# One product per group statistic, an early SiLU table, a second bank for small products, one spreading pass and a new order in a fused convolution, attention and expert kernel

## The chip, the cores and the metric

The kernel runs on one core of one Trainium2 chip. The metric is the device time of one execution in microseconds (us). The kernel before takes 160.03 us, the median of 3 runs (159.5 to 160.67).

## The reference, cut to what matters

The input x is (16, 64, 16, 16) in float32. Two layers follow each other, each added to its input:

```python
# layer 0: split-attention convolution
x = silu(conv1x1(group_norm(hidden, 32)));  x = silu(conv3x3_grouped(group_norm(x, 16)))
x = group_norm(x, 2)
a = silu(conv(max_over_radix(mean_over_8x8_windows(x)))); a = conv(group_norm(a, 8))
out = hidden + group_norm(einsum(x * softmax_over_radix(a), weight), 32)
# layer 1, attention: causal online-softmax average over the 16 images, scores from tanh(fc(LN(h)))
# layer 1, experts: per token 8 experts of three 64 x 64 layers (batch norm folded, relu),
#   summed with softmax(mean(x) @ Wr) as weights, plus the weighted output biases bo
```

## The kernel before, in words

The 16 images are 8 pairs (2 images x 64 channels fill the 128 partitions), worked in two halves k = 0 and 1 of 4 pairs. Every engine runs its own instruction stream. All five streams are written by one list, `ORDER` (L67): each name in it is a stage, and each engine issues its own part of a stage when it comes to that name, so that one entry sets the place of a step on PE, DVE, ACT and POOL at once. Nothing else orders the work; semaphores make each instruction wait for its inputs.

The stages that the text speaks of:

- `warm` and `heat` (L807 to L817): two PE products each on a block of zeros, whose result nobody reads. 16 and 12 of them.
- `gn1`, `gn2`, `gn4`: statistics over channel pairs. `channel_stats` (L494) takes BN_STATS of 4 images on DVE and squares the means; `moments_product` (L785) sums over partitions on PE in four products (L793, L796) into the bank SMALL; `group_finish` (`gn1f`, ...; L473) copies the result on DVE and makes the variance; POOL raises it to the power -0.5 (L312); `group_shift` (L483) makes the offset.
- `gn3`, `gna`, `w2`, `w3`: small products of the window branch, also into SMALL. Each waits until the reader of the one before in `ORDER` has freed the bank (`small`, L774).
- `xnorm`: DVE normalises x (L516), PE makes the 1x1 convolution (L823). `silu0` (L340) is its activation. `norm0`: DVE writes the padded image (L528).
- `conv.0` to `conv.17`: nine taps for each half on PE (L862); `silu.0` to `silu.7` the activations on ACT (L348), `ws` the window sums on DVE (L570) and the sums of squares on ACT (L356).
- `ynorm.0` to `ynorm.3` (L370): ACT normalises four images of y each. `gate` (L618, L623): DVE multiplies by the window weights. `outp` (L874): the output product on PE. `x1` (L377, L633): the residual on ACT and DVE. `tok` (L879): to tokens, centred.
- `ln1`, `hn`, `hch` (L898), `fc` (L904), `score` (L912), `coef`, `att`, `scan`, `cen`, `ln2`, `xt`: attention. `t2`: the context turned back, in the bank TURN (7).
- `l1` (L992), `l2` (L1005), `d1`: the expert layers, 16 duos of experts, their relus on ACT (L428, L436) and for ten halves on DVE (L710).
- `logits`, `wt`, `wb` (L965): routing weights, their transpose on PE, and their spreading to partitions in four products for each pixel half q (L967), copied by ACT (L445). `mix` (L741 on DVE, L1022 on PE): the weighted third layer; before the first `mix` of each q, two products add the biases (L1021). `finish` (L749): the last addition, then the store.

Of the kernel before, what the change touches and what calls it, by code (L numbers as in the profile page):

```python
# [22 lines left out]
ALU = mybir.AluOpType  # L23
# [5 lines left out]
P = 128  # L29
B, C, S = 16, 64, 16  # L30
# [13 lines left out]
STRIP = 32  # L44
EPS = 1e-5
# [13 lines left out]
def columns(cols=COLS):  # L59
# [12 lines left out]
    heat.0 heat.1 w3.0 ws.7 heat.2 heat.3 outp.0 wan.0 gate.0 gate.1 gn4.0 gn4f.0 gn3.1 gn3f.1 x1.0 heat.4 heat.5 win.1 heat.6 tok.0 ln1.0
    heat.7 ln1.1 ynorm.2 w2.1 heat.8 heat.9 heat.10 hn.0 hch.0 hch.1 fc.0 fc.1 hn.1 score.0 gna.1 coef.0 cen.0 att.0 gnaf.1 scan.0 wan.1
    cen.1 ynorm.3 ln2.0 gate.2 w3.1 gate.3 ln2.1 outp.1 xn2.0 xt.0 heat.11 gn4.1 xn2.1 gn4f.1 d1.0 l1.0 xt.1 x1.1 t2.0 l1.1 d1.1 l2.0
    ln1.2 d1.2 ln1.3 tok.1 l1.2 l2.1 t2.1 hn.2 l1.3 l2.2 d1.3 hch.2 xr.0 l1.4 hn.3 hch.3 fc.2 fc.3 xr.1 d1.4 coef.1 att.1 score.1 scan.1
# [7 lines left out]
def conv_attention_experts(nc: bass.Bass, x: bass.AP, params: bass.AP, row_params: bass.AP, conv1_w: bass.AP, out: bass.AP):  # L83
# [6 lines left out]
    with ExitStack() as ctx:  # L90
# [118 lines left out]
        logits_ready, wexp_ready, wt_ready = sem_list("logits_ready", "wexp_ready", "wt_ready")  # L209
        z1_done, h1_ready, h1_by_dve, z2_done = sem_list("z1_done", "h1_ready", "h1_by_dve", "z2_done")  # L210
# [78 lines left out]
        def _(sp):  # L289
# [41 lines left out]
        def _(act):  # L331
# [111 lines left out]
            def weights_copy(q):  # L443
                act.wait_ge(small_ready, SMALL_AT["wb", q])
                A.activation(wb[:, q], bank[SMALL][:].rearrange("p (e n) -> p e n", e=EP), ACT.Copy).then_inc(small_free, 1)  # L445
# [3 lines left out]
                      "xt": x_copies, "spr": lambda k: spread_first_scales(), "l1": relu1, "l2": relu2, "wb": weights_copy}  # L449
            act.wait_ge(early_params_loaded, 16)  # L450
# [7 lines left out]
        def _(dve):  # L458
# [14 lines left out]
            def group_finish(name, n, rows=P, unit=1.0):  # L473
# [678 lines left out]
```

## Time and profile before

| what | us |
|---|---|
| median of 3 runs | 160.03 |
| the profiled execution's own time | 161.2 |
| its span | 159.4 |
| around the span | 1.8 |
| first product of `conv.0` | 20.19 |
| last `conv` done, `silu.4` starts | 40.97 |
| `outp.0` starts | 51.63 |
| `tok.0` starts | 59.65 |
| `outp.1` starts | 83.06 |
| `l1.0` starts | 89.24 |
| last addition (`finish.3`) starts | 156.13 |

The rows give engine times in one profiled execution. An engine's "busy" is the time in which it has an instruction at work, and the chain of waits is the run of work, followed back from the last instruction, that nothing else could have shortened.

### The profile page before, as it was taken

The page shows a single profiled execution, that of the slowest core. Times are in us where ns is not written, and L with a number is a line of the kernel's source. Part 1 is how long each engine was busy: PE and PEld are TensorE (multiplying, and loading weights), DVE is VectorE, ACT ScalarE, POOL GpSimd, SP SyncE. Part 2 cuts the span into 40 slices and gives each one's busy share as a digit, 9 for nine tenths or more (in the row PEclk, how much of TensorE's full clock was granted, in tenths as well). Part 3 has the DMA queues.
Part 4 walks back from the last instruction along what each step waited for, and adds up shares of the span by engine and source line. Part 5 has one row for each costly group of instructions (what it writes and reads, how often), then busy time and mean ns, then how long its engine had stood idle before and what let it go on. Part 6 is the DMA issues. An engine that isn't in the chain of part 4 may idle for free.

```text
span 159.4 us, 2638 instructions
## 1 busy us (share of the span) xinstructions
PE 136.9 (86%) x981; PEld 65.4 (41%) x985; DVE 101.5 (64%) x297; ACT 77.3 (48%) x161; POOL 31.0 (19%) x28
## 2 busy tenths in 40 slices
PE   6997699999318759778869999999999999999991
PEld 2552344344114228348543652466525252222230
DVE  0766574763545663525988479739886449999531
ACT  0009041670797041668030498844588899661400
POOL 7050612004040060700444206100350000000000
PEclk9999999999956975998775999999999999999999
DMA  4980000000000000000000000000000000002222
GB/s 122 405 329 3 0 4 2 4 0 4 2 0 0 0 0 0 0 0 4 0 2 0 0 0 4 0 0 0 0 4 0 0 4 2 0 0 66 70 66 66
DMA packets 3740, 4.63 MB, mean 29 GB/s; under 512 B 208, under 2 KB 3408, under 8 KB 3600
## 3 DMA queue, kind: packets, MB, share of 16 engines
q1 hardware_dynamic: 3584, 4.27, 7.6%
q10 hardware_dynamic: 144, 0.20, 0.6%
q8 instruction: 8, 0.13, 0.4%
q14 instruction: 4, 0.03, 0.1%
HBM read 3.42 MB, written 1.05 MB: 28 GB/s over the span
## 4 chain that ended last, share of the span: by engine, by line
PE 67%; DVE 15%; ACT 11%; POOL 3%; issue 3%; ACTq 0%; POOLq 0%
PE bank L862 11%; PE bank L1022 9%; PE bank L992 8%; PE bank L1005 8%; PE bank L810 4%; PE bank L874 4%; DVE ctxs L685 4%; PE bank L879 3%; ACT y L370 2%; PE bank L912 2%; PE bank L904 2%; ACT x L377 2%; PE bank L793 2%; PE bank L796 2%; DVE y L623 2%
## 5 line engine op out<-in xcount | busy, mean ns | idle before, releaser
L862 PE MATMUL bank<-pad,w 32*64 32x512 f32 x288 | 17.7, 595 | 1.7 <-DVE pad L528 1.7
L1005 PE MATMUL bank<-h,f2s 64*64 64x512 f32 x128 | 17.2, 609 | 0.0
L992 PE MATMUL bank<-xs,f1s 64*64 64x512 f32 x128 | 17.0, 602 | 0.1
L428 ACT ACTIVATE h<-bank,s_bnb 128x512 f32<-128x512 f32 x22 | 14.5, 693 | 3.4 <-PE bank L992 3.4
L810 PE MATMUL bank<-warm 128*128 128x512 bf16 x31 | 9.8, 474 | 1.4 <-POOL warm L314 1.3
L862 PEld LDWEIGHTS bank<-pad,w 32*64 32x64 f32 x288 | 6.8, 130 | 9.8 <-issue 8.9
L348 ACT ACTIVATE y<-bank,par 128x512 f32<-128x512 f32 x8 | 4.9, 686 | 10.9 <-PE bank L862 10.9
L817 PE MATMUL bank<-warm 128*128 128x512 bf16 x21 | 7.7, 497 | 2.8 <-ACT y L348 2.4
L710 DVE TENSOR_SCALAR h<-bank,s_bnb 128x512 f32<-128x512 f32 x10 | 7.5, 747 | 1.1 <-PE bank L992 1.1
L570 DVE TENSOR_REDUCE s_wst<-y 128x8 f32<-128x512 f32 x8 | 5.5, 684 | 4.1 <-ACT y L348 4.0
L934 PE MATMUL bank<-ctxs,par 128*128 128x128 f32 x32 | 6.3, 323 | 1.2 <-DVE ctxs L685 1.2
L340 ACT ACT_TABLE_LOAD x1 | 1.3, 1283 | 12.2 <-PE bank L823 12.2
L992 PEld LDWEIGHTS bank<-xs,f1s 64*64 64x64 f32 x128 | 4.1, 131 | 7.1 <-ACT h L428 4.3
L874 PE MATMUL bank<-y,par 128*64 128x512 f32 x16 | 5.8, 844 | 1.4 <-DVE y L623 1.4
L741 DVE TENSOR_TENSOR y<-y,wb 128x512 f32<-128x512 f32 x8 | 4.9, 683 | 3.3 <-ACT wb L445 3.3
L879 PE MATMUL bank<-par,x 128*128 128x128 f32 x32 | 5.8, 356 | 1.1 <-DVE x L633 0.9
L879 PEld LDWEIGHTS bank<-par,x 128*128 128x128 f32 x32 | 5.3, 261 | 2.9 <-ACT x L377 2.9
L356 ACT ACTIVATE more<-y 128x256 f32<-128x256 f32 x16 | 6.5, 417 | 0.0
L1005 PEld LDWEIGHTS bank<-h,f2s 64*64 64x64 f32 x128 | 3.6, 131 | 6.5 <-issue 3.2
L810 PEld LDWEIGHTS bank<-warm 128*128 128x128 bf16 x32 | 3.7, 124 | 6.0 <-issue 3.3
L685 DVE SCALAR_TENSOR_TENSOR ctxs<-ctxs,s_coefa 128x64 f32<-128x64 f32 x30 | 6.0, 275 | 0.0
L934 PEld LDWEIGHTS bank<-ctxs,par 128*128 128x128 f32 x32 | 4.6, 206 | 3.4 <-DVE ctxs L685 3.4
(251 smaller groups left out, 268.7 us busy)
## 6 DMA issues: line engine op xcount, KB each, us to landing
par<-params SPq DMA_DIRECT2D x1, 1516.0 KB, 8.8
xin<-x SPq DMA_DIRECT2D x4, 256.0 KB, 4.2
out<-act SPq DMA_DIRECT2D x4, 256.0 KB, 2.2
row_par<-row_params SPq DMA_DIRECT2D x2, 160.0 KB, 8.5
w<-conv_w SPq DMA_DIRECT2D x1, 288.0 KB, 5.0
par<-params ACTq DMA_DIRECT2D x1, 193.5 KB, 3.8
```

Source lines behind the costliest of these rows:

```text
L428: A.activation(h1[(2 * m + h) % 4][:], bank[Z1[h]][:], ACT.Relu, bias=tile("bnb", P, 3 * EP)[:, col:col + 1]).then_inc(h1_ready, 1)
L685: V.scalar_tensor_tensor(ctxs[:, k, q, t], before, a_[:, q, t:t + 1], ctxs[:, k, q, t], ALU.mult, ALU.add).then_inc(ctx_ready, 1)
L710: V.tensor_scalar(h1[(2 * m + 1) % 4][:], bank[Z1[1]][:], tile("bnb", P, 3 * EP)[:, col:col + 1], 0.0, ALU.add, ALU.max).then_inc(h1_by_dv ...
L810: T.matmul(bank[TURN][:], warm[:, 0:P], warm[:], start=True, stop=True)
L817: T.matmul(bank[Z1[0]][:], warm[:, 0:P], warm[:], start=True, stop=True)
L862: ins = T.matmul(bank[CONV1[k][2 * j + h]][at:at + C, :], w1[rows, tap, :], pad[rows, b:b + 2, dy:dy + S, dx:dx + S], start=(tap == 0), st ...
L874: ins = T.matmul(bank[CHAIN[k][j]][h * C:(h + 1) * C, :], w("weight")[:, j * C:(j + 1) * C], y[:, b + 2 * h:b + 2 * h + 2, :], start=True, ...
L879: return T.matmul(bank[CHAIN[k][q]][:, i * P:(i + 1) * P], x1[:, k * PK + i, q * P:(q + 1) * P], w("centre"), start=True, stop=True)
L934: ins = T.matmul(bank[CHAIN[k][q]][:, i * P:(i + 1) * P], w("ident"), pair_of(ctxs, k, q, i), start=False, stop=(i == PK - 1))
L992: ins = T.matmul(bank[Z1[h]][to, :], f1s[own, e, to], xs[own, k, q], start=True, stop=True)
L1005: ins = T.matmul(bank[Z2[h]][at:at + C, :], f2s[rows, h, e, :], h1[(2 * m + h) % 4][rows, :], start=True, stop=True)
L1022: T.matmul(bank[OUT[k][q]][h * C:(h + 1) * C, :], wo[:, e, :], held[mixes[m]], start=False, stop=(e == EP - 1)).then_inc(mlp_done, 1)
```

## The change: what it does

Seven edits.

1. `moments_product`: one product of 24 columns (L814 in the changed kernel) in place of four. DVE writes the squared means over the counts of BN_STATS, and `moments_finish` makes the sums with two TENSOR_REDUCE from the bank in place of one copy.
2. ACT runs a SiLU of one column on a constant before it waits for anything of the parameters, so that the table load stands at the start of its stream.
3. `gn3.1`, `w2.1`, `gna.1` and `w3.1` go to the bank TURN with semaphores of their own.
4. `wb`: one pass of eight products, which alternate between q = 0 (partitions 0 to 31, bank SMALL) and q = 1 (partitions 32 to 63, bank TURN). The rows of parameters lie in four strips of 32 partitions in place of two: two more DMAs, and the transposed weights are 128 wide.
5. The biases of both q are added ahead of the first `mix`, four products from four strips into four banks. The first `mix` waits for both spread weights.
6. `ORDER` is new.
7. `STATS_AT` counts by `win` and `wan`, which follow from 6.

```diff
-    warm.0 warm.1 silu0.0 silu0.1 warm.2 spr.0 warm.3 warm.4 warm.5 warm.6 gn1.0 warm.7 warm.8 gn1.1 warm.9 gn1f.0 warm.10 gn1f.1 warm.11
+    silu0.0 warm.0 warm.1 warm.2 warm.3 silu0.1 warm.4 spr.0 warm.5 gn1.0 warm.6 warm.7 warm.8 warm.9 gn1f.0 gn1.1 xnorm.0 warm.10 warm.11
...
-                ins.then_inc(moments_ready, 1)
-                dve.wait_ge(moments_ready, MOMENTS_AT[name])
-                means = raw.rearrange("p n (a t) -> p n a t", a=2)[:, :, :, 1]
-                V.scalar_tensor_tensor(sq, means, float(HALF_PIX), means, ALU.mult, ALU.mult).then_inc(stats_ready, 1)
+                step(ins)
+                parts = raw.rearrange("p n (a t) -> p n a t", a=2)
+                V.scalar_tensor_tensor(parts[:, :, :, 0], parts[:, :, :, 1], float(HALF_PIX), parts[:, :, :, 1],
+                                       ALU.mult, ALU.mult).then_inc(stats_ready, 1)
...
+                V.tensor_reduce(ms[:, 0, :], sums[:, :, :, 1], AX_X, ALU.add)
+                V.tensor_reduce(ms[:, 1, :], sums[:, :, :, 0:3:2], AX_XY, ALU.add).then_inc(small_free, 1)
...
+            act.wait_ge(consts_ready, 1)
+            A.activation(tile("unused", P, 1), minus_half[:, 0:1], ACT.Silu)
             act.wait_ge(early_params_loaded, 16)
...
-            def weights_spread(q):
-                small(("wb", q))
-                pe.wait_ge(rows_loaded, 32)
+            def weights_spread():
+                small(("wb", 0))
+                pe.wait_ge(ctx_added, Q * NK)
+                pe.wait_ge(rows_loaded, 16 * STRIPS)
                 for e in range(EP):
-                    at = (q * EP + e) * P
-                    ins = T.matmul(bank[SMALL][:, e * P:(e + 1) * P], r_("sel")[:, at:at + P], tile("wT", NK * STRIP, P)[0:STRIP], start=True, stop=True)
-                ins.then_inc(small_ready, 1)
+                    for q in range(Q):
+                        at = (q * EP + e) * P
+                        turned = tile("wT", P, P)[q * STRIP:(q + 1) * STRIP]
+                        ins = T.matmul(bank[(SMALL, TURN)[q]][:, e * P:(e + 1) * P], r_("sel", q)[:, at:at + P], turned, start=True, stop=True)
+                ins.then_inc(spread_done, 1)
...
-                if m % (NK * PER_OUT) == 0:
+                if m == 0:
...
+                    pe.wait_ge(wb_ready, Q)
```

What the new order does to ACT between the activations of half 0 and `outp.0`. Before (`y<-bank` is `silu`, `more,s_wsum` the squares, `y<-y` is `ynorm`, `s_wt` the tanh of `w3.0`):

```order
L348 ACTIVATE y<-bank,par 128x512 x4
L356 ACTIVATE more,s_wsum<-y 128x256 x8
L348 ACTIVATE y<-bank,par 128x512 x3
L356 ACTIVATE more,s_wsum<-y 128x256 x2
L362 ACTIVATE s_wth<-s_wh 64x32
L356 ACTIVATE more,s_wsum<-y 128x256 x2
L370 ACTIVATE y<-y,s_gn3v0nb,s_gn3v0r 128x256 x4
L348 ACTIVATE y<-bank,par 128x512
L356 ACTIVATE more,s_wsum<-y 128x256 x2
L370 ACTIVATE y<-y,s_gn3v0nb,s_gn3v0r 128x256 x4
L383 ACTIVATE s_wt<-bank 128x32
```

and now:

```order
L357 ACTIVATE y<-bank,par 128x512 x4
L365 ACTIVATE more,s_wsum<-y 128x256 x8
L380 ACTIVATE y<-y,s_gn3v0nb,s_gn3v0r 128x256 x4
L357 ACTIVATE y<-bank,par 128x512 x3
L365 ACTIVATE more,s_wsum<-y 128x256 x2
L372 ACTIVATE s_wth<-s_wh 64x32
L365 ACTIVATE more,s_wsum<-y 128x256 x2
L357 ACTIVATE y<-bank,par 128x512
L365 ACTIVATE more,s_wsum<-y 128x256 x4
L380 ACTIVATE y<-y,s_gn3v0nb,s_gn3v0r 128x256 x4
L394 ACTIVATE s_wt<-bank 128x32
```

The first `ynorm` has moved ahead of `silu.4`, and the squares of `silu.7` ahead of the tanh.

PE from the end of `conv` to `tok.0`. Before:

```order
L804 MATMUL bank<-s_wmax,par 64x16 x2
L782 MATMUL bank<-s_wr,par 64x16
L817 MATMUL bank<-warm 128x512 x4
L804 MATMUL bank<-s_wan,w3d 128x16 x2
L817 MATMUL bank<-warm 128x512 x4
L874 MATMUL bank<-y,par 64x512 x4
L793 MATMUL bank<-s_gn4v0raw,par 128x8 x2
L796 MATMUL bank<-s_gn4v0rsq,par 128x4 x2
L782 MATMUL bank<-s_wsum,par 128x16
L817 MATMUL bank<-warm 128x512 x6
L879 MATMUL bank<-par,x 128x128 x8
```

and now:

```order
L825 MATMUL bank<-s_wmax,par 64x16 x2
L814 MATMUL bank<-s_wr,par 64x16
L814 MATMUL bank<-s_wsum,par 128x16
L825 MATMUL bank<-s_wan,w3d 128x16 x2
L895 MATMUL bank<-y,par 64x512 x4
L814 MATMUL bank<-s_gn4v0raw,par 128x24
L838 MATMUL bank<-warm 128x512 x6
L825 MATMUL bank<-s_wmax,par 64x16 x2
L838 MATMUL bank<-warm 128x512 x4
L900 MATMUL bank<-par,x 128x128 x8
```

The eight `heat` products ahead of `outp.0` (L874, now L895) are gone, and ten stand between it and `tok.0` (L879, now L900), where six stood.

PE from the transpose of the routing weights on. Before (`s_wsoft` the transpose, `s_wT` with 128x128 the spreading, with 128x512 the biases):

```order
L960 MATMUL bank<-par,s_wsoft 64x128
L945 MATMUL bank<-par,ctxs 128x128 x4
L1005 MATMUL bank<-h_2,f2s 64x512 x2
L1005 MATMUL bank<-h_3,f2s 64x512 x2
L992 MATMUL bank<-xs,f1s 64x512 x4
L967 MATMUL bank<-s_wT,row_par 128x128 x4
L1005 MATMUL bank<-h_0,f2s 64x512 x2
L1005 MATMUL bank<-h_1,f2s 64x512 x2
L992 MATMUL bank<-xs,f1s 64x512 x4
L967 MATMUL bank<-s_wT,row_par 128x128 x4
```

and now:

```order
L981 MATMUL bank<-par,s_wsoft 128x128
L1029 MATMUL bank<-h_0,f2s 64x512 x2
L1029 MATMUL bank<-h_1,f2s 64x512 x2
L991 MATMUL bank<-s_wT,row_par 128x128 x8
L1016 MATMUL bank<-xs,f1s 64x512 x4
L1029 MATMUL bank<-h_2,f2s 64x512 x2
L1029 MATMUL bank<-h_3,f2s 64x512 x2
L1042 MATMUL bank<-s_wT,row_par 128x512 x4
L1043 MATMUL bank<-y,par 64x512 x4
```

The two spreadings stand as one block, and one `l1` and one `l2` stand between it and the biases.

## Rows read from the trace of the kernel before

**Rows 1.** The page, part 1: busy time of each engine, share of the span, instructions.

```profile
PE 136.9 (86%) x981; PEld 65.4 (41%) x985; DVE 101.5 (64%) x297; ACT 77.3 (48%) x161; POOL 31.0 (19%) x28
```

**Rows 2.** Windows: from:to, length, busy us of each engine, granted clock, DMA, GB/s.

```profile
41.00:51.63 10.63, 4.27 (x17) 2.35 (x19) 6.14 (x17) 9.69 (x30) 1.63 (x1) 0.68 0.00 1
...
89.24:156.13 66.89, 66.03 (x458) 27.40 (x457) 48.89 (x113) 42.68 (x73) 7.48 (x5) 1.00 0.04 13
```

**Rows 3.** The chain of waits up to `conv.0`: start us, us, engine, what, line.

```profile
1.32 5.67 PE bank L810 x14
...
10.94 1.14 PE bank L823 x2
...
12.15 1.28 ACT L340
...
15.72 0.58 PE bank L793 x4
16.30 0.46 PE bank L796 x4
...
17.43 1.00 POOL s_gn2v0r L312
...
20.19 4.56 PE bank L862 x80
```

**Rows 4.** Timeline up to 14 us: start, us, engine, line, operation, out<-in, releaser.

```profile
3.25 0.52 SPq L294 DMA_DIRECT2D par<-params  x1
...
4.73 1.41 DVE L501 BATCH_NORM_STATS2 s_gn1v0raw<-xin 128x6 f32<-128x256 f32 x4 [4.73 <-DMA xin<-x]
...
11.64 1.38 DVE L516 TENSOR_SCALAR xnorm<-xin,s_gn1v1r,s_gn1v1nb 128x256 f32<-128x256 f32 x4
```

**Rows 5.** The page, part 6: DMA issues, KB each, us from issue to landing.

```profile
par<-params SPq DMA_DIRECT2D x1, 1516.0 KB, 8.8
```

**Rows 6.** The chain of waits from the last `conv` to `x1.0`.

```profile
40.97 1.84 ACT y L348 x3
...
44.52 1.96 ACT y L370 x4
...
47.05 0.80 ACT more L356 x4
...
51.63 2.15 PE bank L874 x8
...
57.66 1.49 ACT x L377 x3
```

**Rows 7.** Windows of PE alone: busy (instructions), granted clock, DMA.

```profile
44.00:50.50 6.50, 3.35 (x12) 0.50 0.00 0
...
81.50:88.00 6.50, 5.39 (x16) 0.50 0.00 1
```

**Rows 8.** Timeline: offsets of `gn3.0` and `gn3.1`, `tok.0`, `fc`, `outp.1`, `tok.1`.

```profile
38.84 0.17 DVE L486 SCALAR_TENSOR_TENSOR s_gn3v0nb<-s_gn3v0ms,s_gn3v0r 128x8 f32<-128x8 f32 x1 [1.75 <-POOL s_gn3v0r L312]
...
59.65 3.78 PE L879 MATMUL bank<-par,x 128*128 128x128 f32 x16 [0.85 <-DVE x L633]
59.97 0.16 DVE L486 SCALAR_TENSOR_TENSOR s_gn3v1nb<-s_gn3v1ms,s_gn3v1r 128x8 f32<-128x8 f32 x1
...
69.15 1.97 PE L904 MATMUL bank<-xnorm,par 128*128 128x512 f32 x4
...
83.06 3.68 PE L874 MATMUL bank<-y,par 128*64 128x512 f32 x8 [0.90 <-DVE y L623]
...
93.45 2.05 PE L879 MATMUL bank<-par,x 128*128 128x128 f32 x16 [0.21 <-ACT x L377]
```

**Rows 9.** The chain of waits ahead of `l1.0`, and after 127 us (spreading, biases).

```profile
88.00 0.52 PE bank L817
...
127.74 1.08 PE bank L967 x8
...
133.66 1.06 PE bank L1021 x4
```

More of the change, by code:

```diff
@@ L72 @@
[L72 to L75, printed above, removed]
@@ new lines @@
+    gn1f.1 gn2.0 warm.12 warm.13 gn2f.0 silu.0 bn.0 warm.14 warm.15 xnorm.1 silu.1 norm0.0 silu.2 conv.0 conv.1 conv.2 bnf.0 conv.3 conv.4
+    silu.3 gn2.1 conv.5 conv.6 gn2f.1 conv.7 norm0.1 ws.0 ws.1 ws.2 ws.3 conv.8 ynorm.0 s1row.0 conv.9 silu.4 silu.5 conv.10 conv.11
+    s2row.0 conv.12 gn3.0 conv.13 conv.14 gn3f.0 silu.6 win.0 conv.15 conv.16 conv.17 ws.4 w2.0 ws.5 silu.7 ws.6 gna.0 gnaf.0 ws.7 gn3.1
+    wan.0 gn3f.1 gate.0 ynorm.1 gate.1 w3.0 win.1 outp.0 gn4.0 gn4f.0 heat.0 heat.1 ynorm.2 x1.0 heat.2 w2.1 heat.3 ln1.0 heat.4 tok.0
@@ new lines @@
+    heat.5 heat.6 gna.1 heat.7 heat.8 ln1.1 ynorm.3 hn.0 heat.9 hn.1 hch.0 hch.1 fc.0 fc.1 coef.0 score.0 att.0 cen.0 heat.10 heat.11
+    heat.12 gnaf.1 scan.0 wan.1 cen.1 ln2.0 w3.1 heat.13 gate.2 gate.3 ln2.1 outp.1 xn2.0 xt.0 gn4.1 xn2.1 l1.0 gn4f.1 d1.0 xt.1 x1.1 t2.0
+    l1.1 l2.0 tok.1 d1.1 xr.0 ln1.2 d1.2 ln1.3 l1.2 l2.1 l1.3 d1.3 xr.1 hn.2 hn.3 d1.4 l2.2 l1.4 hch.2 hch.3 t2.1 fc.2 fc.3 score.1 coef.1
+    l2.3 cen.2 cen.3 att.1 scan.1 d1.5 l2.4 l1.5 ln2.2 t2.2 d1.6 xn2.2 ln2.3 d1.7 xr.2 d1.8 l1.6 xn2.3 l2.5 l1.7 d1.9 xt.2 l2.6 l1.8 t2.3
@@ L213, in conv_attention_experts, with positions, small_of @@
         mlp_done, res_ready = sem_list("mlp_done", "res_ready")
-        def positions(names):
-            found = [s for s in ORDER if s[0] in names]
+        def positions(names, without=()):
+            found = [s for s in ORDER if s[0] in names and s not in without]
             return {s: i + 1 for i, s in enumerate(found)}
-        SMALL_AT = positions({"gn1", "gn2", "s1row", "s2row", "gn3", "w2", "gna", "w3", "gn4", "score", "logits", "wt", "wb"})
-        MOMENTS_AT = positions({"gn1", "gn2", "gn4"})
-        STATS_AT = positions({"gn1", "gn2", "gn3", "w2", "gna", "w3", "gn4"})
+        second = [s for s in ORDER if s[1] == 1 and s[0] in ("gn3", "w2", "gna", "w3")]
+        SMALL2_AT = {s: i + 1 for i, s in enumerate(second)}
+        SMALL_AT = positions({"gn1", "gn2", "s1row", "s2row", "gn3", "w2", "gna", "w3", "gn4", "score", "logits", "wt", "wb"}, set(second) | {("wb", 1)})
+        def small_of(name):
+            if name in SMALL2_AT:
+                return bank[TURN], small2_ready, small2_free, SMALL2_AT[name]
+            return bank[SMALL], small_ready, small_free, SMALL_AT[name]
+        given = positions({"gn1", "gn2", "gn3", "win", "gna", "wan", "gn4"})
+        STATS_AT = {({"win": "w2", "wan": "w3"}.get(name, name), k): n for (name, k), n in given.items()}
         var_tiles, VAR_AT, at = {}, {}, 0
@@ L380, in radix_tanh @@
             def radix_tanh(k):
-                act.wait_ge(small_ready, SMALL_AT["w3", k])
-                A.activation(tile(f"wt{k}", P, BK * WIN), bank[SMALL][:, 0:BK * WIN], ACT.Tanh, scale=0.5).then_inc(small_free, 1)
+                area, ready, free, at = small_of(("w3", k))
+                act.wait_ge(ready, at)
+                A.activation(tile(f"wt{k}", P, BK * WIN), area[:, 0:BK * WIN], ACT.Tanh, scale=0.5).then_inc(free, 1)
             def squares(n):
@@ L752, in _ @@
             stages = {
-                "gn1": gn1_stats, "gn1f": lambda k: group_finish(("gn1", k), PK, unit=HALF_PIX), "xnorm": normalise_x,
-                "gn2": gn2_stats, "gn2f": lambda k: group_finish(("gn2", k), PK, unit=HALF_PIX), "norm0": normalise_0,
+                "gn1": gn1_stats, "gn1f": lambda k: moments_finish(("gn1", k), PK), "xnorm": normalise_x,
+                "gn2": gn2_stats, "gn2f": lambda k: moments_finish(("gn2", k), PK), "norm0": normalise_0,
                 "bn": lambda k: batch_norm_variances(), "bnf": lambda k: fold_weights(),
@@ L803, in two_order_product @@
                     cols = slice(j * n // 2, (j + 1) * n // 2)
-                    ins = T.matmul(bank[SMALL][0:rows, cols], matrices[j], rhs[:, cols], start=True, stop=True)
-                ins.then_inc(small_ready, 1)
+                    ins = T.matmul(area[0:rows, cols], matrices[j], rhs[:, cols], start=True, stop=True)
+                ins.then_inc(ready, 1)
             def warm_up(n):
```

116 lines of the change are left out of this document (58 added, 58 removed).

## The prediction, on record before the changed kernel ran

> **What bounds the kernel now.** I read the page first, then windows by stage, then the chain of waits in order of time, and the timeline for what that chain does not show. The page gives PE 86% of the span [rows 1], which is an average over two different kernels. From `l1.0` at 89.24 to 156.13 us PE works 66.03 of 66.89 us at a granted clock of 1.00 [rows 2]: there only PE's own work counts, and PE instructions taken out shorten the time. From the last `conv` to `outp.0` PE works 4.27 of 10.63 us at a mean clock of 0.68, while ACT works 9.69 [rows 2]: there a chain through ACT sets the time, and a step taken off ACT's queue counts in full. The part up to `conv.0` at 20.19 is a chain too: PE, DVE, ACT, POOL in turn [rows 3]. The run of `conv` between is PE without a gap.
>
> So the time falls where the change shortens the chain up to 20.19, ACT between 40.97 and 51.63, and PE's own work after 89.24. I go through these in order and carry one number, how much earlier a point comes.
>
> **Up to `conv.0`.** Four things happen.
>
> First, `gn1`. Before, PE ran 14 warm-ups in 5.67 us and conv0 began at 10.94 [rows 3]. Now twelve stand there; at 5.67 / 14 = 0.41 each they end at 6.2. BN_STATS ends at 6.14 [rows 4], and a small dependent DVE step costs about 0.2 (0.17 busy [rows 8] and the hand-over), so the product waits for DVE and ends near 6.9. Two reductions and two small steps (0.7) and POOL's power (1.0) give the first scale at 8.7; DVE fills this with BN_STATS of the other half (1.41) and reaches `xnorm.0` at 9.35; two of its four pieces take 0.7. conv0 begins at 10.1, 0.8 earlier.
>
> Second, the table. ACT loads it from 12.15 for 1.28 us when conv0's first product is already there [rows 3]. Now it is loaded while ACT has nothing else: 1.28 gone. By the Trainium skill, "ScalarE: Activation LUTs", section "What ACT_TABLE_LOAD costs", a switch costs the load and about as much again for a drain, 2.66 us in all. The trace shows the load alone on the chain [rows 3]; by the page the gain would be 1.38 larger. I go by the row.
>
> Third, the product of `gn2.0`. Before, two groups of 0.58 and 0.46 [rows 3]. Now one product of 24 columns in two passes. No row has that shape; the four records of the `gn1` matrix in 0.58 bound it from above, half of them, 0.29, from below; I take 0.38, which saves 0.66. Against this DVE's squaring (0.2), which used to lie beside PE's first products, stands ahead of the product, and a second reduction (0.1) replaces part of a copy. Net 0.3 gained; the ends are 0 and 0.5.
>
> Fourth, order. `xnorm.1` (1.38 [rows 4]) ran before in the shadow of conv0 and of the table load. Now it stands on DVE between `gn2f.0` and `norm0.0`, beside POOL's 1.00 us [rows 3]. With the two offsets (0.2 each) and `bn.0` it lasts 2.05 against the 1.3 of POOL and one offset: 0.7 lost. `bn.0`, ahead of it, waits for the large parameter transfer, issued at 3.25 [rows 4] and 8.8 us on its way [rows 5], so landed at 12.1; it is asked for near 15. The two added row transfers are issued behind it. They cost nothing unless they hold it back by 3 us.
>
> Sum: 0.8 + 1.28 + 0.3 - 0.7 = 1.7. `conv.0` starts at 18.5.
>
> **The run of `conv`.** PE stays without a gap, and `gn2.1` inside it falls from the same four products to one: 0.6. The other steps keep their place in it. Last `conv` 1.7 + 0.6 = 2.3 earlier: 38.65.
>
> **ACT to `outp.0`.** Before, ACT did three `silu` (1.84), squares, the small tanh, `ynorm.0` (1.96), `silu.7`, squares, `ynorm.1`, the tanh of `w3.0`, without a gap [rows 6]. Now `ynorm.0` stands ahead of `silu.4`. Its offset, at 38.84 before [rows 8], comes 2.3 earlier as well, at 36.6, so it runs from 36.6 to 38.6 in time in which ACT was idle: 1.96 taken off the chain. The squares of `silu.7` (0.80 [rows 6]), which ran behind the tanh, now stand ahead of it. Net 1.16. The branch beside it, `gna.0` to the product `w3.0`, reaches PE near 45.6 and ends before the tanh at 46.5. The second bank keeps `gn3.1` from waiting for `gna.0`; it hides under ACT. `outp.0` 2.3 + 1.15 = 3.4 earlier, at 48.2.
>
> **`outp.0` to the end of `tok.0`, and the clock.** The eight `heat` products ahead of `outp.0` are gone. The trace: after PE had nearly nothing to do, the clock stood at 0.50 from 44.0 to 50.5, and at 0.50 again from 81.5 to 88.0 [rows 7]. That is 1.2 in place of 2.4 GHz. The same four products took 2.15 us for `outp.0` behind the `heat` products [rows 6] and 3.68 us for `outp.1` at the low clock [rows 8]. By the Trainium skill, "TensorE: Matmul & The Clock Gate", section "HAM oscillation — how this bites in real kernels", work behind an idle stretch starts cold; the trace agrees (3.68 against 2.15), and it speaks against this change. PE has only small products between 39 and 48.2 now, so I take the low clock: 1.53 lost, 0.33 of it returned by `gn4.0`'s single product. `win.1`, six small DVE steps of some 0.2 each, which before began at 59.97 [rows 8], now stands ahead of `gn4.0`; it hides under the slower product (at the high clock it would cost 0.4). `x1.0` 3.4 - 1.2 = 2.2 earlier: 55.5.
>
> Then ten `heat` products instead of six, in a stretch of 4 us that they fill at the low clock. I expect the clock high for most of `tok.0`. `tok.0` took 3.78 us low, `tok.1` 2.05 high [rows 8]: between 0 and 1.7 gained, I take 1.0. End of `tok.0` 3.2 earlier.
>
> **To `l1.0`.** `ln1`, `hch`, `fc`, `score`, `att`, `scan` keep their sequence. More `heat` products stand between; ten in front of `hch.0` fit under POOL's two powers at the high clock, six behind `cen.0` under DVE's `att`. Ahead of `l1.0` a `heat` product (0.52 [rows 9]) is gone and `gn4.1` is shorter: 0.75 gained. If the added `heat` products keep the clock up for `outp.1`, 0.9 more. I take 0.9 (ends 0 and 1.7). `l1.0` 4.1 earlier: 85.1.
>
> **After `l1.0`.** Two spreadings of 1.08 [rows 9] become one of eight products. The pairs come from different partitions and go to different banks, as the two bias products already do, which take 1.06 together [rows 9]. I take 1.1 for the block (serial would be 2.16). The two bias groups of 1.06 become one of four products, again 1.06 (serial 2.1). Saved 1.08 + 1.06 = 2.14. The second half's chain is less well filled: `t2.1` no longer stands between `l2.1` and `l1.3`, where a relu on DVE comes last, and `xt.2` and the routing products wait a little for ACT. Going through the queues with the durations above I find 0.5 more idle time. Net 1.65. The last products, the addition and the store stay.
>
> **Sum.** 3.2 + 0.9 + 1.65 = 5.75. The profiled execution's own time is 161.2 (span 159.4 and 1.8 around it), 1.2 above the median of the runs. By its own time 155.45; from the median, 160.03 - 5.75 = **154.3**.
>
> **The rivals.**
>
> *The PE-bound part gives back its saving* (chance 0.20). The spreading does not overlap, or ACT and DVE, 42.68 and 48.89 us busy of 66.89 [rows 2], put gaps into PE as the new order packs them. Then 2.14 or more is lost: 156.4. For it: `wb` must wait for ACT behind `l2.10`, and the first `mix` for both copies. Against it: the bias rows overlap already.
>
> *The clock stays low from `conv` to `l1.0`* (0.12). Then `tok.0` gains nothing (1.0), `fc` at 1.97 [rows 8] doubles (+1.97), and half of `hch` (0.5): 157.8. For it: 9 us without large work. Against it: the same `heat` products lifted it by 51.
>
> *The clock is high throughout* (0.05): 1.2 at `outp.0` and 0.8 at `outp.1` on top: 152.3.
>
> *The drain of the page is real here* (0.05): 154.3 - 1.38 = 152.9.
>
> *Slower* (0.03): routing weights too late. No `mix` may start before both copies; only `l1.12` and `l2.11` stand between. Whatever the second half's chain (`tok.1`, `score.1`, `scan.1`, `ln2.3`, `xt.3`, `logits`) comes late is added whole. From 5.75 + 1.6 late it is slower by over 1%; at 7.5, 161.8. Against it: I find that chain at most 0.5 later than PE.
>
> The forecast keeps 0.55.
>
> **How the numbers follow.** No change can be told within 1%, that is above 158.4 and below 161.6. Faster by over 1%: 0.55 + 0.20 + 0.05 + 0.05 and 0.07 of the low-clock case = 0.92; within 1%: its other 0.05; slower: 0.03. The range reaches down to the two better cases (152.3 with 0.3 for small steps) and up to the low clock's 157.8: 152.0 to 158.0.
>
> **What would show it right or wrong.** Table load before 3 us; conv0 at 10.1; `conv.0` at 18.5; `ynorm.0` ended when `silu.4` starts at 38.7; `outp.0` at 48.2, 3.7 us long at clock 0.50; `tok.0` near 2.8 us; `l1.0` at 85; spreading block 1.1 and bias block 1.06 us; last addition 150.4. I am wrong if `ynorm.0` still runs after `silu.4`, if `outp.0` starts after 50, or if PE idles over 1.5 us after `l1.0`.

## The result, and the profile after

The changed kernel takes 155.06 us, the median of 4 runs (154.75 to 156.44). The kernel before, run beside it, takes 160.35 us (159.5 to 161.81, 4 runs). The ratio is 0.9678 with a 95% interval of 0.9584 to 0.9772: faster by some 3%. The forecast was 154.3 within 152.0 to 158.0.

The profiled execution of the changed kernel took 154.75 us with a span of 152.8, so its span is 6.6 us shorter than that of before, while the medians differ by 5.3. Both kernels scatter by 1.1 to 1.4%, and the experiments show that the clock has a part in it. In this text a median counts every run, while a ratio leaves out the runs over 1.5% above the fastest of their kernel (three of six in the variant with edit 1 alone, and five of six with the early load alone, which therefore has no ratio).

The page of the changed kernel, part 1 and the clock's line of part 2. Against [rows 1] PE has lost 7.3 us of work and DVE and ACT have gained 0.6 and 0.7; the clock has two low places, at slices 12 to 15 and at slices 21 and 22.

```profile
PE 129.6 (85%) x951; PEld 58.6 (38%) x953; DVE 102.1 (67%) x305; ACT 78.0 (51%) x162; POOL 31.0 (20%) x28
...
PEclk9999999999965559999968999999999999999999
```

The chain of waits of the changed kernel from the start to `conv.0` (start us, us, engine, what, line), which answers to [rows 3]:

```profile
1.21 1.28 ACT L462 ACT_TABLE_LOAD   x1 [1.21 <-PEq L1167]
```

```profile
1.31 5.04 PE bank L831 x12
6.46 0.39 PE bank L814 x2
...
9.93 2.00 PE bank L844 x4
11.96 0.70 ACT act L349
...
13.79 0.39 PE bank L814 x2
...
15.02 1.17 DVE xnorm L542 x4
16.51 1.40 DVE pad L554 x4
18.05 4.56 PE bank L883 x80
```

The first row is from the timeline of ACT, not from the chain: the table load lies at 1.21 us, beside the warm-up products, and no load stands between conv0 (L844) and its activation (L349) any more. The product for a group statistic has two records (two passes) of 0.39 us together, at `gn1.0` (6.46) and `gn2.0` (13.79). `xnorm.1` (L542) is on the chain at 15.02, as its new place says.

The chain from the offset of `gn3.0` to `tok.0`, which answers to [rows 6]:

```profile
36.05 0.18 DVE s_gn3v0nb L500
36.25 2.07 ACT y L380 x4
38.32 0.58 ACT y L357
...
42.95 1.64 POOL s_gnav0r L321
...
45.36 1.02 PE bank L825 x4
46.40 0.21 ACT s_wt L394
...
48.33 3.69 PE bank L895 x8
...
53.17 0.59 PE bank L814 x2
```

`ynorm.0` (L380) ends just when `silu.4` (L357) starts; the last `conv` ends at 38.16, so `ynorm.0` has no room to spare there. From there to `outp.0` (L895) the chain is no longer ACT's: it goes through DVE, POOL and the small product `w3.0` (L825), and the tanh (L394) waits for that.

Windows of the changed kernel (from:to, length, busy us of each engine, granted clock, DMA, GB/s): from `l1.0` to the last addition, which answers to the second row of [rows 2], and below it PE alone where the clock is low, for [rows 7].

```profile
84.08:149.55 65.47, 64.02 (x458) 26.55 (x457) 49.34 (x117) 42.55 (x73) 7.52 (x5) 1.00 0.03 9
```

```profile
44.00:57.00 13.00, 8.88 (x26) 0.50 0.00 1
77.50:81.50 4.00, 4.00 (x16) 0.57 0.02 4
```

After `l1.0` PE's work fell by 66.03 - 64.02 = 2.01 us and its idle time rose from 0.86 to 1.45, so the stretch is 1.42 shorter. The clock is low once from 43.5 to 57.2 and once for 4 us; before it was low from 43.5 to 51, 57.5 to 64.5, 74.5 to 78.5 and 81 to 88.5, in half-microsecond windows.

The timeline of PE has `tok.0` and `outp.1`, two of the products of [rows 8]:

```profile
57.83 1.96 PE L900 MATMUL bank<-par,x 128*128 128x128 f32 x16
...
79.66 2.61 PE L895 MATMUL bank<-y,par 128*64 128x512 f32 x8
```

And the chain from the transpose's neighbours to the biases, for [rows 9]:

```profile
122.48 0.69 ACT more L447
123.21 1.09 PE bank L1029 x8
124.30 1.09 PE bank L991 x16
...
127.27 1.07 PE bank L1042 x8
```

Sixteen records of spreading now take 1.09 us where eight took 1.08. The two rows ahead show one of the new gaps: an `l2` (L1029) waits for its relu on ACT.

### The profile page after: what moved, and what is told of

It is laid out like the page before. It is cut to its first block, busy times and chain, and to the rows that moved or that the text cites. A ratio compares the mean times of both kernels' runs of the same rounds, so it can differ in the third digit from the quotient of the medians.

```text
span 152.8 us, 2584 instructions
## 1 busy us (share of the span) xinstructions
PE 129.6 (85%) x951; PEld 58.6 (38%) x953; DVE 102.1 (67%) x305; ACT 78.0 (51%) x162; POOL 31.0 (20%) x28
## 4 chain that ended last, share of the span: by engine, by line
PE 60%; DVE 24%; ACT 6%; POOL 5%; issue 4%; POOLq 0%
PE bank L1043 10%; PE bank L883 8%; PE bank L1016 8%; PE bank L1029 7%; DVE ctxs L713 4%; PE bank L831 3%; PE bank L933 2%; PE bank L895 2%; PE bank L900 2%; DVE y L651 2%; PE bank L925 2%; PE bank L838 2%; PE bank L814 2%; ACT y L380 1%; DVE s_wst L596 1%
## 5 line engine op out<-in xcount | busy, mean ns | idle before, releaser
L1029 PE MATMUL bank<-h,f2s 64*64 64x512 f32 x128 | 17.1, 603 | 0.3 <-ACT more L447 0.2
L349 ACT ACTIVATE act<-bank,par 128x512 f32<-128x512 f32 x4 | 2.8, 689 | 13.1 <-PE bank L844 13.0
L895 PE MATMUL bank<-y,par 128*64 128x512 f32 x16 | 6.3, 928 | 2.0 <-DVE y L651 2.0
L414 ACT ACTIVATE square<-bank 128x512 f32<-128x512 f32 x4 | 2.4, 597 | 10.0 <-PE bank L955 10.0
L357 ACT ACTIVATE y<-bank,par 128x512 f32<-128x512 f32 x8 | 4.9, 679 | 4.5 <-PE bank L883 4.5
L955 PEld LDWEIGHTS bank<-ctxs,par 128*128 128x128 f32 x32 | 5.1, 221 | 4.5 <-DVE ctxs L713 4.3
L1029 PEld LDWEIGHTS bank<-h,f2s 64*64 64x64 f32 x128 | 4.0, 132 | 6.7 <-issue 4.3
L380 ACT ACTIVATE y<-y,s_gn3v0nb,s_gn3v0r 128x256 f32<-128x256 f32 x8 | 4.1, 591 | 4.1 <-DVE s_gn3v0nb L500 4.1
```

The source lines that it names most:

```text
L895: ins = T.matmul(bank[CHAIN[k][j]][h * C:(h + 1) * C, :], w("weight")[:, j * C:(j + 1) * C], y[:, b + 2 * h:b + 2 * h + 2, :], start=True, ...
L955: ins = T.matmul(bank[CHAIN[k][q]][:, i * P:(i + 1) * P], w("ident"), pair_of(ctxs, k, q, i), start=False, stop=(i == PK - 1))
L1029: ins = T.matmul(bank[Z2[h]][at:at + C, :], f2s[rows, h, e, :], h1[(2 * m + h) % 4][rows, :], start=True, stop=True)
```

## The experiments

Each was timed against the kernel before on the same chip: 161.06 us (17 runs) for the first four, 161.05 (10) for the next four, 161.31 (11) for the last four. The last four (without the early load, `t2` moved back, warm-ups in `ln2.0`, and the best version) ran on another chip than the first eight, and the changed kernel itself was not run beside them. Edit 3, the second bank, was not tried by itself; it is in every variant that starts from the changed code. "Marks" are start times in the profiled execution of the variant, and since the clock scatters from run to run, a mark behind 43 us carries that with it.

### Parts of the change put into the kernel before

The early table load alone:

```diff
+            act.wait_ge(consts_ready, 1)
+            A.activation(tile("unused", P, 1), minus_half[:, 0:1], ACT.Silu)
             act.wait_ge(early_params_loaded, 16)
```

> The kernel before with the early SiLU of one column alone. My theory: the load of 1.28 us leaves the chain and nothing takes its place, so conv.0 starts at 18.9 (20.19 before) and the time falls by 1.28 to 159.1 (from 160.35). Rival (a drain as long as the load goes with it, as the Trainium skill has it): 2.66 gone, conv.0 at 17.5. Rival (the load is hidden by something else): no change.

Measured: median 161.21 (158.41 to 162.0, 6 runs), before 161.06. From conv0's first product to `conv.0` 8.11 us in place of 9.25: 1.14 saved, close to the 1.28 of the load. `conv.0` is at 19.37, only 0.82 earlier than in [rows 3], since conv0 itself began 0.32 later. And the median did not move, where 159.1 was expected. The timeline of PE in this variant shows where it went, beside [rows 8] and the 2.15 of [rows 6]:

```profile
50.80 3.68 PE L876 MATMUL bank<-y,par 128*64 128x512 f32 x8 [0.26 <-DVE y L625]
```

`outp.0` ran at the low clock, 1.5 us longer, and `l1.0` started at 89.92, later than before. Of the six runs the one with a mean granted clock of 0.945 took 158.41, the five with 0.914 to 0.925 took 160.8 to 162.0. The kernel before took 159.3 and 159.5 at 0.946, and 160.1 to 162.8 in its runs at 0.914 to 0.925. The step on the chain is shown, and in the profiled execution the clock takes it back; that it does so in the others is not shown.

Edit 1 alone (one product per statistic):

```diff
-                ins.then_inc(moments_ready, 1)
+                step(ins)
...
+                V.tensor_reduce(ms[:, 0, :], sums[:, :, :, 1], AX_X, ALU.add)
+                V.tensor_reduce(ms[:, 1, :], sums[:, :, :, 0:3:2], AX_XY, ALU.add).then_inc(small_free, 1)
```

> The kernel before with one product per group statistic alone, old order. My theory: conv.0 0.3 earlier, gn2.1 inside the run of conv 0.6 shorter (so silu.4 starts 0.9 earlier, at 40.1), gn4.0 0.3 and gn4.1 0.5 on the chain: 1.7 in all, 158.7. Rival (DVE's squaring ahead of the product and the two reductions eat it): silu.4 starts 0.6 earlier from the run of conv alone and the time falls by 0.6.

Measured: 158.58 (156.55 to 160.5, 6 runs), ratio 0.9782 (0.9712 to 0.9853). `conv.0` at 19.45, 0.74 earlier than [rows 3], and from there to `silu.4` 20.25 us in place of 20.78: 0.53 for `gn2.1`, where 0.6 was reckoned. Together 1.3 on the chain. The median fell by 2.5, more than that, but the profiled execution was only 1.75 shorter than that of before (159.45 against 161.2), with 0.45 gained between `silu.4` and `l1.0` (87.52) and nothing behind. There `outp.0` took 2.87 (2.15 before) and `tok.0` 2.12 (3.78 before), and the runs with a mean clock of 0.945 and more took 156.6 to 157.7, those with 0.91 to 0.92 took 159.5 to 160.5.

Edits 4 and 5 alone (one spreading pass, biases of both halves together), in the old order:

```diff
+                for e in range(EP):
+                    for q in range(Q):
+                        turned = tile("wT", P, P)[q * STRIP:(q + 1) * STRIP]
...
+                if m == 0:
+                    pe.wait_ge(wb_ready, Q)
```

> The kernel before with the one spreading pass and the biases of both halves ahead of the first mix, old order. My theory: products of two partition strips into two banks overlap, block of sixteen records in 1.1 us, bias block of eight in 1.06, so PE has 2.14 less to do after l1.0 and the last addition comes 2.1 earlier: 158.2. Rival (no overlap): the block takes 2.16, the bias block 2.1, no change in time. Rival (ACT and DVE cannot follow): blocks short, but the gain turns into PE idle time after the first mix.

Measured: 160.78 (159.37 to 161.83, 12 runs), ratio 1.0005 (0.9962 to 1.0048): no change in time, where 158.2 was expected. Its window from `l1.0` to the last addition:

```profile
88.70:154.85 66.15, 64.31 (x458) 26.14 (x457) 49.09 (x116) 42.52 (x73) 7.48 (x5) 1.00 0.04 13
```

The overlap is as foreseen (blocks of 1.09 and 1.07, PE's work 1.72 less than in [rows 2]), but idle time rose from 0.86 to 1.84, so 0.74 is left, less than this measurement can tell. Its chain of waits shows where it comes from: the relus (L438) wait for the `l2` (L1010) behind the block, and the next `l2` waits for them with only one `l1` to fill the time:

```profile
127.19 1.09 PE bank L972 x16
128.28 1.06 PE bank L1010 x8
...
129.95 0.68 ACT more L438
130.63 1.16 ACT h L430 x2
...
131.88 1.09 PE bank L997 x8
```

```profile
130.68 1.09 PE L1010 MATMUL bank<-h,f2s 64*64 64x512 f32 x8 [0.53 <-ACT more L438]
```

The kernel before has neither this gap of 0.53 nor a like one of 0.38 at 147.52; together they are 0.91 of the 0.98 of added idle time.

All of the changed code with the old order:

```diff
-    silu0.0 warm.0 warm.1 warm.2 warm.3 silu0.1 ...
+    warm.0 warm.1 silu0.0 silu0.1 warm.2 spr.0 ...
```

> The changed kernel with the order of the kernel before: all the code, none of the order. My theory: the code is worth 1.28 + 1.7 + 2.1 = 5.1 at most, of which some goes again into waits that the old order does not fill: 155.6. The new order is then worth only 0.5 on top, since its ynorm.0 (1.2) is given back at outp.0 by the low clock (1.5) and regained at tok.0 and outp.1. Rival (the order carries the gain): 157.5 or more here.

Measured: 157.37 (155.71 to 157.95, 6 runs), ratio 0.9785 (0.9718 to 0.9851). The changed kernel, run again in the next set, has 0.9665 (0.9629 to 0.9702): with the order goes a difference of 1.2% or about 2 us, four times what I had given it. The marks do not show that much. The order gives 0.6 at `conv.0` (18.63 against 18.05), 0.5 between `silu.4` and `outp.0` (10.66 against 10.10) and 0.66 after `l1.0` (66.13 against 65.47), but between `outp.0` and `tok.0` it loses 1.85, for here, behind eight warm-up products, `outp.0` runs at the high clock:

```profile
49.61 2.12 PE L895 MATMUL bank<-y,par 128*64 128x512 f32 x8 [0.26 <-DVE y L651]
```

`tok.0` starts at 57.26, 0.57 ahead of the changed kernel, and `l1.0` at 84.48, between the two profiles of the changed kernel (84.08 and 84.65). The last addition is at 150.61, against 149.55 and 150.13: 0.5 to 1.1 for the order, near what I had said. At least part of the rest of the 2 us goes with the clock: the two runs of this variant at 0.945 took 155.7 and 155.8 and its four at 0.912 to 0.934 took 156.9 to 158.0, while the changed kernel's ten runs stood at 0.933 to 0.955. Whether the new order's own warm-up products earn that is not shown.

The first of the marks is a surprise that the variant's chain explains:

```profile
4.99 1.44 DVE s_gn1v0raw L515 x4
...
6.62 1.32 DVE s_gn1v1raw L515 x4
...
10.09 1.38 DVE xnorm L542 x4
...
11.58 1.38 DVE xnorm L542 x4
12.96 1.43 DVE s_gn2v0raw L515 x4
```

In the old order DVE takes the BN_STATS of both halves before it finishes `gn1.0`, and conv0 starts at 10.88 and not at 9.93; 0.28 of these 0.95 is the input, which came later in this execution (4.99 against 4.71). `xnorm.1` in its old place costs little here: it ends when BN_STATS of `gn2.0` start, at 12.96, and these start 1.95 behind conv0 in the changed kernel, which would be 12.83. Its new place costs 0.35 behind the product. So the gain ahead of `conv.0` comes from taking `gn1.0` first. Whether `xnorm.1` could then have stayed was not run; by an estimate it could not, since its scale in the changed kernel is ready only at 12.16 (POOL, from 11.15 for 1.01), and with an offset and its own 1.38 it would hold BN_STATS, which start at 11.88, to about 13.7.

### Parts taken out of the changed kernel

The changed kernel once more, as the base of this set.

> The changed kernel once more, so that the others of this set stand beside it on the same chip. Both theories: 155.1, with a scatter of some 1 us that goes with the mean granted clock (in the first three experiments runs of one kernel at a mean clock of 0.912 and at 0.945 lay 2 to 4 us apart).

Measured: 155.35 (154.91 to 156.0, 6 runs), ratio 0.9665 (0.9629 to 0.9702). Its profile has `outp.0` at 48.46 for 3.68 us, `outp.1` for 1.94 and `l1.0` at 84.65, and 65.48 us from there to the last addition.

`ynorm.0` back behind `ws.5`:

```diff
-    ... conv.8 ynorm.0 s1row.0 ... w2.0 ws.5 silu.7
+    ... conv.8 s1row.0 ... w2.0 ws.5 ynorm.0 silu.7
```

> The changed kernel with ynorm.0 put back behind the squares of silu.6 (ws.5), the rest as it is. My theory: its 1.96 us on ACT stand on the chain again, outp.0 starts 1.9 later than in the changed kernel (silu.4 to outp.0 12.0 in place of 10.1), 157.0. Rival (DVE and POOL set this stretch, ACT has slack): outp.0 later by under 0.7, 155.5.

Measured: 157.47 (156.31 to 157.65, 6 runs), ratio 0.9784 (0.9747 to 0.9821). The chain of this variant is ACT's again, without a gap to the tanh:

```profile
41.79 1.97 ACT y L380 x4
43.76 0.57 ACT y L357
44.33 1.60 ACT more L365 x8
45.93 1.97 ACT y L380 x4
...
47.90 0.21 ACT s_wt L394
```

The tanh starts at 47.90 in place of 46.53 in the base: 1.37 later, though 1.97 of work came back. The rest fits a wait: in the changed kernel ACT stands idle ahead of the tanh, which this row of its timeline gives as 0.52 us:

```profile
46.40 0.20 ACT L394 ACTIVATE s_wt<-bank 128x32 f32<-128x32 f32 x1 [0.52 <-PE bank L825]
```

So moving `ynorm.0` brought 1.4 to 1.5 of its 1.97, and the branch through POOL and `w3.0` is the bound for the rest. The medians differ by 2.1, more than the mark. In the profile `l1.0` comes 1.68 later than in the base, and the stretch behind it is 0.58 longer, with one low place of the clock in it that the base does not have:

```profile
86.33:152.39 66.06, 65.07 (x458) 27.71 (x457) 49.38 (x117) 42.57 (x73) 7.52 (x5) 0.97 0.03 9
```

The early table load taken out again:

```diff
-            act.wait_ge(consts_ready, 1)
-            A.activation(tile("unused", P, 1), minus_half[:, 0:1], ACT.Silu)
```

> The changed kernel without the early SiLU. In the first set the early load alone made conv.0 0.8 earlier and the time no shorter, with a lower mean clock. My theory: the load is worth its 1.28 on the chain and the first set only lost it again to the clock (outp.0 at 1.2 GHz where it had 2.4 before); here, where outp.0 runs at 1.2 GHz either way, taking it out costs 1.1 to 1.3: conv.0 at 19.3, time 156.6. Rival (it is worth nothing in time): 155.4. Rival (load and drain, 2.66): 158.0.

Measured: 156.14 (155.92 to 156.31, 6 runs), ratio 0.9667 (0.9627 to 0.9708). In its chain the load is back:

```profile
10.14 1.14 PE bank L842 x2
...
11.35 1.28 ACT L349
12.65 0.70 ACT act L349
...
19.37 0.65 PE bank L881 x2
```

`conv.0` starts 1.2 to 1.3 later than in the two profiles of the changed kernel, and `l1.0` at 85.42, 0.8 to 1.3 later. In the medians it is 0.8 (156.14 against 155.35), in the ratios nothing; the two belong to different sets and chips, and half a per cent is not told apart that way. What is shown is the load's 1.2 on the chain, with no second part as long as itself: by the Trainium skill, "ScalarE: Activation LUTs", section "What ACT_TABLE_LOAD costs", the switch would have cost 2.66 us, and both variants contradict it here.

### The clock

All `heat` products taken out:

```diff
-    ... gn4.0 gn4f.0 heat.0 heat.1 ynorm.2 x1.0 heat.2 w2.1 heat.3 ln1.0 heat.4 tok.0
+    ... gn4.0 gn4f.0 ynorm.2 x1.0 w2.1 ln1.0 tok.0
```

> The changed kernel without any heat product (the 28 behind conv). My theory: the clock stays at 1.2 GHz from the end of conv to the experts, tok.0 3.78 (1.96), fc 3.6 (1.97), outp.1 3.68, so l1.0 comes 3 to 4.5 us later: 158.5. Rival (the small products and outp.0 lift the clock by themselves): at most 1 us later, 156.

Measured: 158.94 (158.48 to 159.09, 6 runs), ratio 0.9887 (0.9855 to 0.9919), so these products are worth 3.6 us. `outp.0` is the same (48.42, 3.68 us); the clock then stays at 0.50 until 61 and is low again from 64 to 71:

```profile
57.83 3.40 PE L900 MATMUL bank<-par,x 128*128 128x128 f32 x16 [3.44 <-DVE x L661]
```

In the changed kernel the same `tok.0` starts at the same time and takes 1.96, as its clock rose at 57.2. The ten products ahead of it are not the whole of this: in two profiles of variants that have the same code up to here (`t2` moved back, and warm-ups in `ln2.0`) the clock rose at 56.5 and at 51.8, the second ahead of all of them. What the six runs show is that without any of the 28 the mean clock is 0.88 to 0.90 in every one, and 0.933 to 0.955 with them.

Warm-up products between the last `conv` and `outp.0`, twenty in all; those named 30 and up go into the bank TURN, and the first of these waits for `silu.4`:

```diff
-    ... ws.4 w2.0 ws.5 silu.7 ws.6 gna.0 gnaf.0 ws.7 gn3.1
+    ... ws.4 w2.0 heat.30 heat.31 heat.32 heat.33 heat.34 ws.5 silu.7 ws.6 gna.0 heat.35 heat.36 heat.37 gnaf.0 ws.7 gn3.1
...
-    ... w3.0 win.1 outp.0 gn4.0 gn4f.0 heat.0
+    ... w3.0 heat.0 heat.20 win.1 outp.0 gn4.0 gn4f.0 heat.24
```

> The changed kernel with warm-ups from the end of conv to outp.0: five pairs into the bank TURN behind w2.0, three pairs behind gna.0, two pairs behind w3.0. My theory: the clock stays at 2.4 GHz over this stretch, outp.0 lasts 2.15 in place of 3.68, but win.1 on DVE then comes first, so x1.0 is only 0.8 earlier: 154.3. Rival (the warm-ups run at 1.2 GHz and delay gna.0 and w3.0): outp.0 starts 1 or more later, 156. Rival (the clock at outp.0 is worth its full 1.5): 153.6.

Measured: 154.23 (153.02 to 155.7, 6 runs), ratio 0.958 (0.9538 to 0.9621). The hope for `outp.0` failed: in the profile it still takes 3.68 us and the clock is low from 46 to 57. But low from 46, not from 43.5, and that reaches `w3.0`, the product on the chain:

```profile
45.30 0.59 PE L825 MATMUL bank<-s_wan,w3d 65*128 65x16 f32 x4 [0.62 <-DVE s_wan L637]
```

0.59 where it took 1.02, and `outp.0` starts at 47.86: from `conv.0` to it 0.4 less than in the two profiles of the changed kernel (29.88 against 30.28 and 30.30). Two of the six runs had a mean clock of 0.977 and took 153.0 and 153.9.

Three warm-up products in the first context addition (`ln2.0`), where PE waits for DVE:

```diff
+                    if n == 0 and i < PK - 1:
+                        T.matmul(bank[Z1[0]][:], warm[:, 0:P], warm[:], start=True, stop=True)
```

> The changed kernel with one warm-up product behind each of the first three context products of ln2.0, in gaps of 0.29 us in which PE waits for the scan. My theory: outp.1 comes at 2.4 GHz in most runs (1.9 to 2.15 us, in the profiled runs so far 2.61, 1.94, 3.68), the low clock that begins at 77 to 81 is gone, l1.0 up to 0.5 earlier and the mean clock at 0.955: 155.0. Rival (the products delay the scan's consumers): ln2.0's square later by 0.3, 155.7.

Measured: 154.69 (154.48 to 154.9, 6 runs), ratio 0.9578 (0.9538 to 0.9619). In this profile no low stretch is left behind 52 us, and `outp.1` takes 2.22 us:

```profile
79.37 2.22 PE L895 MATMUL bank<-y,par 128*64 128x512 f32 x8 [0.83 <-DVE y L651]
```

All six runs lie within 0.4 us, as do those of the variant without the early load. But the marks do not credit these three products with the gain: from the end of `tok.0` to `l1.0` 24.30 us pass here, 24.29 and 24.73 in the two profiles of the changed kernel, and `tok.0` starts 0.35 to 0.39 earlier, ahead of the edit, where the clock rose at 51.8. With no changed kernel in this set, what the edit is worth stays open.

### The tail, and the best version

`t2.1` and `t2.3` back at the places where they fill PE:

```diff
-    l1.2 l2.1 l1.3 ... hch.2 hch.3 t2.1 fc.2 ... l1.8 t2.3 ... wt.0 l2.10
+    l1.2 l2.1 t2.1 l1.3 ... hch.2 hch.3 fc.2 ... l1.8 ... wt.0 t2.3 l2.10
```

> The changed kernel with t2.1 put back between l2.1 and l1.3, and t2.3 between wt.0 and l2.10. My theory: PE's idle time after l1.0 falls from 1.47 by 0.6 (0.2 ahead of l1.3, 0.4 and more ahead of l2.10), l1.0 to the last addition 64.9 in place of 65.5, time 154.8. Rival (the second half's chain through DVE and ACT ends the waits elsewhere): 65.5 again.

Measured: 155.9 (154.99 to 156.62, 6 runs), ratio 0.964 (0.9588 to 0.9693): no gain. Its window is 65.85 us with 64.25 of PE's work, 0.38 longer than in the changed kernel.

```profile
85.54:151.39 65.85, 64.25 (x458) 26.48 (x457) 49.32 (x117) 42.71 (x73) 7.51 (x5) 1.00 0.03 9
```

The two gaps of 0.22 and 0.21 that I meant to fill are gone, and one of 0.51 has come ahead of another `l2`, which waits for ACT. I read this as idle time that ACT's queue carries, which moving PE's filling only moves.

The two warm-up edits and this one together:

> The warm-ups to outp.0 (154.2 alone), those in ln2.0 and the two moved turns together. My theory: the gains add up, 1.1 + 0.3 + 0.6 from 155.35: 153.4. Rival (the clock gains exclude each other): 154.2.

Measured: 154.43 (153.3 to 154.72, 6 runs), ratio 0.9553 (0.9507 to 0.9598), at mean clocks of 0.966 to 0.989. Its window after `l1.0` is 65.78, as long as with the filling alone. Against the expected 153.4 the additions do not add up; that with the clock nearly whole the chain is what is left is an argument, not a finding. Three variants have intervals at or below 0.9621, where the changed kernel's begins at 0.9629: this one, the warm-ups ahead of `outp.0`, and those in `ln2.0`. Only the warm-ups ahead of `outp.0` ran in the same set as the changed kernel, and for them a gain of about 1% is shown (154.23 against 155.35). For the other two it stands across sets, and the variant without the early load warns of that: its ratio equals the changed kernel's, though its chain is 1.2 longer. The warm-ups without the filling in one kernel were not tried.

## Why the prediction was right

By its own steps, gains counted in the profiled executions (predicted, measured):

| how much earlier | predicted | measured |
|---|---|---|
| `conv.0` | 1.7 | 2.14 |
| `silu.4` | 2.3 | 2.74 |
| `outp.0` | 3.4 | 3.30 |
| `x1.0` | 2.2 | 1.90 |
| end of `tok.0` | 3.2 | 3.64 |
| `l1.0` | 4.1 | 5.16 |
| after `l1.0` alone | 1.65 | 1.42 |
| sum | 5.75 | 6.58 |

**Up to `conv.0`.** conv0 at 9.93 (10.1 said), the load at 1.21 (before 3 said), the product 0.39 (0.38 said). The first term gave 1.01 and not 0.8. The third held: from the end of BN_STATS (15.59 before, 13.43 now) to the variance (17.34 and 14.84) lie 1.41 us in place of 1.75, the 0.3 that was said. The fourth was too dear: from the variance's last step (14.68 and 0.16) to `norm0.0` (16.51) lie 1.67 us against 1.32 before, a loss of 0.35, not 0.7. It reckoned each small step at 0.2, but `bn.0` and the offset of `gn1.1` together kept `xnorm.1` only 0.18 behind the variance (14.84 to 15.02).

**ACT to `outp.0`.** The start of `outp.0` was right by 0.1, by two errors that cancel: `silu.4` came 0.4 earlier than said, and the step behind it gave 3.30 - 2.74 = 0.56 in place of 1.16. The sentence that failed is that the branch "reaches PE near 45.6 and ends before the tanh at 46.5". By the letter it holds, for the branch reached PE at 45.36 and ended at 46.38; but ACT was free at 45.89 (43.82 and 2.07), and not at 46.5 (the prediction's own sum gives 46.25), so the branch and not ACT set the tanh, and ACT waited 0.52. `w3.0` took 1.02 us at the low clock. Where warm-up products held the clock up it took 0.59, which would have ended it at 45.95 and left ACT almost no wait. With this wait 0.56 + 0.52 = 1.08 of ACT's work is accounted for. I had foreseen the low clock for the large product and not priced the small one, which becomes the bound.

**The clock.** `outp.0` at 3.68 us as said, the price 1.53 paid in full. `tok.0` was sized at a gain of 1.0, between 0 and 1.7; it gained 1.82, as the clock rose at 57.2, ahead of it. From there to `l1.0` 0.9 was taken, with 1.7 as the upper end, and 1.52 measured, 1.07 of it in `outp.1` (2.61 in place of 3.68). That size is in part luck: with the same code up to it `outp.1` took 2.61, 1.94 and 3.52 in three profiles. By the Trainium skill, "TensorE: Matmul & The Clock Gate", section "HAM oscillation — how this bites in real kernels", work behind an idle stretch starts cold. The traces agree so far: `outp.0` took 3.62 us or more in all seven profiles without warm-up products ahead of it. With such products it took 2.12 in three, 2.87 in one, and still 3.62 to 3.68 in three (the early load alone, the twenty warm-ups, and the best version), so they do not secure the high clock.

**After `l1.0`.** The overlap was right: 1.09 and 1.07 for the blocks, PE's work 2.01 less against 2.14. The added idle time was put at 0.5 and measured 0.59. That the net is 1.42 and not 1.65 is these two together. The 1.45 of idle time stood just under the 1.5 from which the prediction would have called itself wrong.

**The total.** By profiled executions the sum was 0.8 too small; by medians 5.3 came (5.7 in the repeat), and the forecast from the median was 0.8 too low. Both are smaller than what the clock does to one kernel between runs.

Of the rivals, the one in which the tail gives its saving back holds for the spreading alone in the old order (1.0 of 1.72 given back), and not with the new order. The drain did not show. Neither clock rival came about in full. The clock moved time both ways: 1.53 lost at `outp.0`, 1.82 gained at `tok.0` and 1.07 at `outp.1`.

Several expectations before the runs failed in the time: the early load alone and the spreading alone left the median where it was, the moved `t2` brought nothing, and the best version missed the sum of its parts. I gave the order half a microsecond and the code the rest; by the medians the order brings about 2, by the marks 0.5 to 1.1, and at least part of what lies between goes with the clock.

## What to carry to other kernels

When a step moves forward, ask again for the place of each step behind it: with `gn1.0` taken first, `xnorm.1` would by an estimate no longer have fitted where it stood. Where the clock falls, reprice every product on the chain, the small ones too. Where PE waits anyway, warm-up products are worth a try: all 28 taken out cost 3.6 us, and twenty more gained 1.1. Judge an edit of 1 us on such a kernel by its marks in the trace and by the mean granted clock of each run together, since the median alone can hide it (early load, 1.14 saved, median unchanged) or enlarge it (edit 1, 1.3 on the chain, 1.75 in the profiled execution, 2.5 in the median). And run the base again in every set: across sets and chips half a per cent cannot be told.

## What the runs showed of the hardware

The time of one kernel goes with its mean granted clock, though not strictly: in the early-load variant 158.4 us at 0.945 and 161.2 to 162.0 at 0.914 and 0.915, in the variant with edit 1 156.55 at 0.956, 160.5 at 0.922 and 159.45 at 0.913. Which of TensorE's two levels, 1.2 or 2.4 GHz, a stretch gets differs between executions of the same code: `outp.1` took 2.61 us in one profile of the changed kernel and 1.94 in another, and the low stretch that holds `outp.0` ended at 57.2, 56.6, 56.5 and 51.8 us in four profiles with the same code up to there.

A float32 product of 24 columns takes 0.37 to 0.39 us in two passes at the high clock and 0.59 at the low one. Products that read different strips of 32 partitions and write different banks overlap fully: 16 records in 1.09 us, where 8 from one strip took 1.08; four bias products from four strips took 1.07, where two took 1.06.
